# A layer with attention and feed-forward on one core: in the second half, the split of the moved q placed behind the key-value mask, the first Relu and the norms of the next half

## What is computed

```
xn  = layernorm(x)
qkv = xn @ qkv_w + qkv_b          # q, k, v with 16 heads of 16 channels
q, k = q / |q|, k / |k|           # per token and head
kv  = k^T v                       # per head, 16 x 16, over the 1024 tokens of a batch
att = (q @ kv) @ proj_w + proj_b
ffn = relu(xn @ W1 + b1) @ W2 + b2
out = x + att + ffn
```

## Time and profile before

| | us |
|---|---|
| runs | 572.85, 574.08, 574.26 |
| median | 574.08 |
| the profiled execution | 573.04 |
| its span, first to last instruction | 571.3 |
| TensorE busy in it | 561.3 (98%) |
| VectorE busy | 415.0 (73%) |
| ScalarE busy | 283.0 (50%) |
| GpSimd busy | 119.6 (21%) |
| DMA: 45.36 MB moved | mean 79 GB/s |

### The profile page before, as it was taken

One profiled execution on the slowest core, in us unless ns is written; L12 is line 12 of the kernel. 1 busy time (PEld: TensorE's weight loads), 2 busy tenths in 40 slices (PEclk: granted clock), 3 DMA queues, 4 the chain that ended last, 5 costly groups with the idle time before them and its releaser, 6 DMA issues.

```text
span 571.3 us, 8956 instructions
## 1 busy us (share of the span) xinstructions
PE 561.3 (98%) x2722; PEld 477.5 (84%) x2722; DVE 415.0 (73%) x807; ACT 283.0 (50%) x516; POOL 119.6 (21%) x148
## 2 busy tenths in 40 slices
PE   8999979999999999999999999999999999999997
PEld 7788868888888888888888888888888888888896
DVE  6887868767787777858679496676868767784755
ACT  3586453555436554355633746345563555433421
POOL 2522423310152020520205202132023300150100
PEclk9999998999999999999999999999999999999999
DMA  8322135254433536135461354514444252424423
GB/s 287 119 83 48 30 80 95 36 105 79 95 58 83 101 74 103 15 86 94 85 94 18 85 94 85 85 30 93 86 85 73 40 95 48 76 35 74 111 38 75
DMA packets 141398, 45.36 MB, mean 79 GB/s; under 512 B 133314, under 2 KB 136386, under 8 KB 141380
## 3 DMA queue, kind: packets, MB, share of 16 engines
q1 hardware_dynamic: 139264, 44.61, 38.9%
q10 hardware_dynamic: 2116, 0.53, 0.6%
HBM read 20.98 MB, written 8.39 MB: 51 GB/s over the span
## 4 chain that ended last, share of the span: by engine, by line
PE 91%; DVE 3%; ACT 2%; SPq 2%; DMA 1%; issue 1%; DVEq 0%; ACTq 0%
PE o_bank L1038 11%; PE o_bank L1039 11%; PE o_bank L1040 11%; PE w_bank L1040 10%; PE w_bank L1038 10%; PE w_bank L1039 10%; PE v_bank L1038 6%; PE v_bank L1039 6%; PE v_bank L1040 6%; PE g_bank L1038 3%; PE g_bank L1040 3%; PE g_bank L1039 3%; SPq L308 2%; PE kv_bank L1159 1%; ACT w_hi L475 0%
## 5 line engine op out<-in xcount | busy, mean ns | idle before, releaser
L840 DVE SCALAR_TENSOR_TENSOR h_lo<-w_bank,h_hi 128x512 fp32r<-128x512 f32 x128 | 87.4, 683 | 34.1 <-ACT h_hi L540 32.6
L540 ACT ACTIVATE h_hi<-w_bank 128x512 fp32r<-128x512 f32 x128 | 76.4, 597 | 71.9 <-PE w_bank L1040 70.0
L1040 PE MATMUL w_bank<-xT_hi,w_lo 128*128 128x512 f32 x254 | 100.5, 396 | 0.0
L1038 PE MATMUL w_bank<-xT_hi,w_hi 128*128 128x512 f32 x254 | 100.2, 394 | 0.0
L1039 PE MATMUL w_bank<-xT_lo,w_hi 128*128 128x512 f32 x254 | 100.2, 394 | 0.0
L1038 PE MATMUL o_bank<-h_hi,w_hi 128*128 128x512 f32 x240 | 95.1, 396 | 0.0
L1039 PE MATMUL o_bank<-h_lo,w_hi 128*128 128x512 f32 x240 | 94.9, 396 | 0.0
L1040 PE MATMUL o_bank<-h_hi,w_lo 128*128 128x512 f32 x240 | 94.6, 394 | 0.0
L372 POOL TENSOR_TENSOR xn_lo<-xn,xn_hi 128x256 fp32r<-128x256 f32 x56 | 41.6, 742 | 228.5 <-ACT xn_hi L475 220.0
L387 POOL TENSOR_TENSOR y_sb<-y_sb,y_rows 128x256 f32<-128x256 f32 x56 | 53.1, 952 | 130.6 <-DVE y_rows L879 108.1
L518 ACT ACTIVATE qk_sq<-v_bank 128x512 f32<-128x512 f32 x64 | 38.3, 599 | 77.8 <-PE v_bank L1040 77.4
(11 more groups left out here) (188 smaller groups left out, 988.6 us busy)
## 6 DMA issues: line engine op xcount, KB each, us to landing
qT_lo<-blocks SPq DMA_DIRECT2D x256, 32.0 KB, 1.9
x_sb<-x SPq DMA_DIRECT2D x15, 512.0 KB, 3.9
y_sb<-x SPq DMA_DIRECT2D x60, 128.0 KB, 3.5
out<-y_sb SPq DMA_DIRECT2D x58, 128.0 KB, 2.7
xT_raw<-blocks SPq DMA_DIRECT2D x224, 32.0 KB, 1.9
y_sb<-w SPq DMA_DIRECT2D x4, 256.0 KB, 5.1
w_raw<-w SPq DMA_DIRECT2D x1, 768.0 KB, 9.1
x_sb<-x SPq DMA_DIRECT2D x2, 256.0 KB, 2.9
```

What stands on the lines that cost most here:

```text
L540: nc.scalar.activation(h_hi[:, j % RING, :], w_bank[j % 2][:], ACT.Relu).then_inc(h_done, 1)
L840: nc.vector.scalar_tensor_tensor(h_lo[:, r, :], w_bank[j % 2][:], 0.0, h_hi[:, r, :].bitcast(F32), ALU.max, ALU.subtract).then_inc(h_lo_do ...
L1038: nc.tensor.matmul(to, left[0], right[0], start=first, stop=False, skip_group_check=shared)
L1040: return nc.tensor.matmul(to, left[1], right[0], start=False, stop=last, skip_group_check=shared)
```

## The change

In the second half only, the split of this half's own moved q (side 1) changes its place. On ScalarE, `qT_high(1, 1)` moves from behind `qT_high(0, 0)` to behind `qk_sqrt(2)` and ahead of `m_high(0)`; it passes `qk_out(2, 0, 2)`, `h_high(1, 7)`, `qk_out(2, 0, 3)`, `h_high(2, 0)` and `qk_sqrt(2)`. On VectorE, `qT_low(1, 1)` moves from behind `qT_low(0, 0)` to behind `norms(2)` and ahead of `m_low(0)`; it passes `sum_squares(2, 2)`, `mask_kv(0)`, `h_low(1, 7)`, `sum_squares(2, 3)`, `bound(2)`, `h_low(2, 0)` and `norms(2)`. The other halves keep their order. SP, GpSimd and TensorE have the same program as before.

```diff
@@ scalar, half
                 if is_second(s):
                     qT_high(0, 0)
                 if ahead:
-                    qT_high(s, u)
+                    if not is_second(s):
+                        qT_high(s, u)
                     qk_out(s + 1, 1 - u, 2)
...
                     qk_out(s + 1, 1 - u, 3)
                     h_high(s + 1, 0)
                     qk_sqrt(s + 1)
+                if is_second(s):
+                    qT_high(s, u)
                 if u == 1 and ahead:
                     m_high(b)
@@ vector, half
                 if is_second(s):
                     qT_low(0, 0)
                 if ahead:
-                    qT_low(s, u)
+                    if not is_second(s):
+                        qT_low(s, u)
                     sum_squares(s + 1, 2)
                     if u == 1:
                         mask_kv(b)
...
                     bound(s + 1)
                     h_low(s + 1, 0)
                     norms(s + 1)
+                if is_second(s):
+                    qT_low(s, u)
                 if u == 1 and ahead:
                     m_low(b)
```

## The result

| | before | after |
|---|---|---|
| median of the runs timed together | 573.75 (572.85 to 574.26, 4 runs) | 569.17 (568.84 to 569.29, 4 runs) |
| ratio, 95% interval | | 0.9921 [0.9904, 0.9938] |
| the profiled execution | 573.04 | 569.29 |
| its span | 571.3 | 567.5 |

The kernel is faster by 0.8%. From profiled execution to profiled execution it is 573.04 - 569.29 = 3.75 us, which is the forecast's sum; by the medians it is 4.58. Where the other 0.8 come from is the subject of the last experiments.

The account below looks back on a forecast made before the run. TensorE, busy 98%, bounds the kernel; its 3.7 us kv_lo wait and clock drop go. Attention gains 4.31 us, the later y wait leaves 3.75: 573.04 to 569.3 profiled, 574.08 to 570.3 median; 8-in-10 range 568.0 to 572.2.

Parts of the forecast that it names:

- the forecast's sum: Whole program: TensorE 3.75 us earlier at the third half's first down product, kept to the end; profiled execution 573.04 to 569.3.
- The steps: Second half into third: mask starts 77.87, kv_lo ready 79.99, m's products 81.26, m_lo ends 85.76, attention could start 85.82.
- The two new waits: TensorE waits 1.07 us for m_lo before the attention, then 0.46 for the y copy before the third half's first down product.
- 91.56 is a DMA landing that nothing here moves: Landing of x's moves ahead of ScalarE's split; argued against the rival that 4.4 to 5.5 us are gained, chance 0.10.
- The clock: TensorE behind the short new waits: no clock drop taken, since only the 3.65 us idle piece was followed by 0.50.
- the start-up stretch: TensorE from 7.90 to 12.00 us: idle 1.10 of 4.10 us in short pieces, with the clock staying at 1.00.
- that rival: Clock falls at the short waits too, costing 1.54 us: 2.77 or 2.2 gained, median 571.3 to 571.9; chance 0.12.
- lost to the clock: Kernel before, twelve products after 85.89 on TensorE: 4.34 us where 2.80 at full clock, so 1.54 lost.
- 574.08 - 3.75: Forecast median 570.3 us: the median of the three runs shown, 1.04 above the profiled execution, less the gain.
- Downstream: Behind the third half's y: VectorE lags TensorE by 0.99 us more, costed at nothing, at most 0.99; the advance stays.
- 0.97 us in hand: Third half's gather: k_lo ended at 104.56, gather started at 105.53; this margin was expected to vanish, give or take 0.05.

Follow-up runs that it names:

- the last experiments: Kernel before with 28 extra products filling TensorE's idle stretch ahead of m's products, 572.57 us; and three more profiled executions of the kernel before, 573.12, 574.51 and 573.05.
- the two edits alone: On the changed kernel: m's split ahead of the moved q's split, 568.95 us; ScalarE's y copies ahead of its split of x, 569.06; both edits, 567.91.
- doubling the wait: Changed kernel with VectorE's division of k for the third half put between the moved q's split and m's low part: 571.62 us, ratio 0.9972 to the kernel before.
- the filled idle stretch: Kernel before with 28 extra products of 256 columns on TensorE ahead of m's products in the second half: 572.57 us against 572.99, ratio 0.9991.
- only the step that the wait list names: Kernel before with only VectorE's mask moved, right behind the split of the first moved q, both splits left in place: 570.50 us, ratio 0.9956.

## Why the prediction was right

**The steps.** Each place on the path came within 0.1 us of its forecast: mask at 77.87, measured 77.89; kv_lo 79.99, 80.01; m's products 81.26, 81.33; m_lo's end 85.76, 85.76; attention 85.82, 85.86; first down product of the third half 93.37 without the slow first product, 93.34. The predicted 3.75 us for the profiled execution are 3.75 measured (573.04 - 569.29). This worked because every input of the moved steps was in the trace with its own time, and because the sum was taken as the shift of a place on TensorE's timeline and not as a sum of the waits removed. That it agrees to the last digit is luck: x's moves landed 15.61 us after the first split in the profiled execution before and 15.59 after, where other executions of kernels with the same SP program had down to 14.78, and an earlier landing would have given up to 0.4 us more.

**The two new waits** were named, sized (1.07 and 0.46; measured 0.86 as listed, which is 1.0 from the last down product's slot to the attention, and 0.26, or 0.43 from slot to slot) and are in series, as the two edits alone (0.44, 0.33) and together (1.48) show. What was mis-stated is how fixed the second is: "91.56 is a DMA landing that nothing here moves" holds for its cause, but it moves by up to 0.8 us by itself from execution to execution.

**The clock.** It stayed up behind the short waits in all nine runs, as I had taken from the start-up stretch. The Trainium skill, "TensorE: Matmul & The Clock Gate", section "A second HAM failure mode: psum-queue depth-cycling", says that frequent short idles between groups of matmuls can make the clock swing. These nine runs, whose profiles have idles of 0.9 and up to 0.3 us there, do not show it. But doubling the wait brought the drop in six runs of eight, so the margin was smaller than the text, which set 1.07 us against 3.65, made it look. The price in that rival, 1.54, is what the drop then cost (1.53).

**Where the text was wrong without harm.** It called the 1.54 us "lost to the clock". In the kernel before about 0.5 of it was on the path, which the filled idle stretch showed (0.4 us gained instead of my 1.54). The sum did not suffer only because it compared places. The gain of 3.75 is thus some 3.1 to 3.3 from waits and some 0.4 to 0.7 from the clock, by two estimates: the runs of the kernel before with a mean clock of 0.998 or more have a median of 572.37 (572.37 - 569.29 = 3.1, 573.04 - 572.37 = 0.7), and the kernel with the stretch filled has 572.57 (3.3 and 0.5).

**The median.** Taken as 574.08 - 3.75 it gave 570.3, and 569.17 was measured, 1.1 us lower and inside the range. The three runs shown included 574.08 and 574.26, which by their times, held against the later runs, are probably executions with the long drop; the median over 46 runs is 573.08, and 573.08 - 3.75 = 569.33 is the changed kernel's 569.3 (median of nine). The profiled execution was the better base, and I moved off it.

**Downstream** I expected the gather to keep nothing of its 0.97 us in hand, "or more if GpSimd's additions ... cover less of VectorE's work". The second holds. VectorE's and GpSimd's timelines after, against the earlier trace rows:

```profile
94.55 1.25 DVE L702 TENSOR_TENSOR xT_lo<-xT_raw,xT_hi 128x512 fp32r<-128x512 f32 x2
...
99.47 1.38 DVE L702 TENSOR_TENSOR k_lo<-qk_even,k_hi 128x1024 fp32r<-128x1024 f32 x1
```
```profile
95.47 8.47 POOL L387 TENSOR_TENSOR y_sb<-y_sb,y_rows 128x256 f32<-128x256 f32 x8 [19.18 <-DMA y_sb<-x]
```

The two subtractions of xT_lo took 2.13 us when GpSimd's additions lay over them, and 1.25 now that they mostly come before. k_lo ends at 100.85 and the gather starts at 101.79: 0.94 in hand, as before.

## What to carry to other kernels

When an engine stands for a transfer, list what is queued behind it on every engine and ask of each entry whether it needs the transfer; here five steps of ScalarE and seven of VectorE did not, and moving the waiting pair on both engines paid where moving VectorE's half alone, or only the step that the wait list names, paid nothing and two thirds. Size such a change as the shift of one place on the limiting engine's timeline, with every new wait recomputed in order, since waits in series do not add and a low clock can lie over a wait that would be there anyway. After the edit, look at once for the next wait in the series: two that were worth 0.4 and 0.3 us alone were worth 1.5 together.

## What the runs showed that I had not expected

The granted clock can fall behind an idle stretch of 2.0 us (six of eight runs), and did not behind 0.9 us (none of nine), nor behind the 1.27 us in the opening of the profile after. Behind the stretch of 3.3 to 3.7 us in the kernel before it fell in all four profiles and in most runs, but apparently not in all (9 of 46 have a mean clock of 0.998 or more; none of these was profiled). A drop lasted about 3.4 us in five profiles and about twice that in one, where 1.25 us more came through. The split of the moved x, two subtractions on VectorE, took 1.25 to 1.29 us in the six profiles where it came mostly ahead of GpSimd's additions, and 1.80 to 2.13 in the eight where it lay beside them. No run changed only that, so the additions as the cause are argued, not shown.
